# A first attention whose query and value projections move into the tail of a turn, and a feed-forward stage whose first low part is made before the first product is scaled

## The reference

```
x = x + tanh(g_xattn[0]) * window_attention(layernorm(x), ctx)   # 8 heads, window 16, 1x1 projections q, k, v, o
x = x + tanh(g_ffn[0])   * quantized_ffn(layernorm(x))           # int8 fake-quantized w1, gelu, w3
x = x + tanh(g_xattn[1]) * lane_attention(layernorm(x), ctx)     # q = layernorm(x) @ Wq.T, k, v from ctx
x = x + tanh(g_ffn[1])   * swiglu_ffn(layernorm(x))              # with low-rank additions
```

## Time and profile before

| | before |
|---|---|
| median of 3 runs | 3655.55 us |
| lowest, highest | 3651.84, 3661.02 us |
| the profiled execution | 3649.41 us |
| its span | 3647.7 us |
| PE, DVE, ACT, POOL busy | 90%, 39%, 24%, 10% of the span |
| mean granted TensorE clock | 0.954 of full speed |
| first attention | 0 to 475.45 us |
| fused feed-forward and queries | 475.45 us to about 980 us |

### The profile page before, as it was taken

The page is one execution under the profiler, slowest core; times in us unless marked ns, Lnnn a source line. Parts: engine busy times, 40 slices in busy tenths (PEclk is TensorE's granted clock), DMA queues, the critical chain, the costliest instruction groups (busy, mean ns, idle before and its releaser), DMA issues. The chain is left out here.

```text
span 3647.7 us, 52611 instructions
## 1 busy us (share of the span) xinstructions
PE 3294.2 (90%) x21047; PEld 2507.2 (69%) x21076; DVE 1433.3 (39%) x2021; ACT 889.8 (24%) x1232; POOL 349.3 (10%) x304
## 2 busy tenths in 40 slices
PE   5888855999799997899999669999999999999999
PEld 2454442777678885566666458888888888778777
DVE  6666657777220002677676362111121122310000
ACT  1222243333121112555454221111111111200000
POOL 2000000000000001232222111111111111000000
PEclk9999977999789998999999879999999999999999
DMA  4656451221232223121121243222222222544443
GB/s 95 131 115 126 89 185 35 70 70 59 76 104 69 61 60 110 70 85 58 64 80 63 66 131 103 91 94 94 94 94 94 94 94 82 202 145 132 141 141 104
DMA packets 339441, 352.61 MB, mean 97 GB/s; under 512 B 154352, under 2 KB 261472, under 8 KB 337264
## 3 DMA queue, kind: packets, MB, share of 16 engines
q1 hardware_dynamic: 339312, 350.79, 31.1%
HBM read 215.23 MB, written 126.97 MB: 94 GB/s over the span
## 5 line engine op out<-in xcount | busy, mean ns | idle before, releaser
L2213 PE MATMUL g_ps<-g_xs,g_wt 128*128 128x512 f32 x4128 | 957.2, 392 | 0.0
L2213 PEld LDWEIGHTS g_ps<-g_xs,g_wt 128*128 128x128 f32 x4128 | 774.3, 189 | 160.7
L2269 PE MATMUL g_ps<-g_wd,g_h 128*128 128x512 f32 x2016 | 463.0, 392 | 6.8 <-DMA g_h<-g_hidden 4.1
L2269 PEld LDWEIGHTS g_ps<-g_wd,g_h 128*128 128x128 f32 x2016 | 381.1, 189 | 88.1 <-DMA g_h<-g_hidden 4.7
L2131 DVE SCALAR_TENSOR_TENSOR g_act_out<-g_ps,g_g,g_act_out 128x512 f32<-128x512 f32 (+1 forms) x88 | 66.1, 751 | 691.4 <-ACT g_act_out L2063 691.4
L2063 ACT ACTIVATE g_act_out<-g_ps 128x512 f32<-128x512 f32 (+1 forms) x88 | 52.6, 598 | 655.7 <-PE g_ps L2213 655.7
L1263 PE MATMUL kv_gps<-kv_xh,kv_wh 128*128 128x512 f32 x512 | 200.5, 392 | 0.0
L1263 PE MATMUL kv_gps<-kv_xl,kv_wh 128*128 128x512 f32 x512 | 199.3, 389 | 0.0
L1263 PE MATMUL kv_gps<-kv_xh,kv_wl 128*128 128x512 f32 x512 | 199.3, 389 | 0.0
L1008 PE MATMUL f_gps<-f_xt,f_qwh 128*128 128x256 f32 x1024 | 194.2, 290 | 1.4 <-DVE f_xt L887 1.4
L1611 PEld LDWEIGHTS a_tps<-a_ident,a_e 128*128 128x128 f32 x1024 | 113.4, 144 | 104.6 <-issue 90.5
(11 more groups left out here) (247 smaller groups left out, 4257.6 us busy)
## 6 DMA issues: line engine op xcount, KB each, us to landing
g_h<-g_hidden SPq DMA_DIRECT2D x176, 256.0 KB, 2.6
g_hidden<-g_h SPq DMA_DIRECT2D x84, 512.0 KB, 2.7
kv<-kv_y SPq DMA_DIRECT2D x16, 1024.0 KB, 5.7
a_kv<-kv SPq DMA_DIRECT2D x16, 1024.0 KB, 4.9
g_xb<-x SPq DMA_DIRECT2D x24, 512.0 KB, 4.0
g_down<-g_raw SPq DMA_DIRECT2D x22, 512.0 KB, 2.8
g_raw<-g_down SPq DMA_DIRECT2D x22, 512.0 KB, 4.3
g_raw<-in_L_ffn_gate_w_dram SPq DMA_DIRECT2D x21, 512.0 KB, 4.0
```

The costliest lines, as they stand in the source:

```text
L2213: w = pe.matmul(gps[:, c % 2, m, :], wt[m][i][:, l, ks], xs[c][:, r, k, :], start=(k == 0 and a == 0), stop=(k == NK - 1 and a == 2))
L2269: w = pe.matmul(to, tile[:, p % RING, l, cols], wd[f][:, r, os], start=(f == 0 and a == 0), stop=False)
```

## The change

In the first attention, PE makes only the two key projections at the head of a turn, between the first scores; the two query projections come after the last `attend`, the values after the transposes of the output, and the product by `Wo` (now a function `final`) last. ACT follows that order, and its exponential comes after the copy of the output instead of before. DVE runs `normalize` between the maxima (`largest`) and their subtraction (`shift`); its two `value` steps move from between the selects to before and after `sums`. SP spreads the keys ahead of the store of the values. In the fused stage, `low(b - 1, 0)` stands ahead of `scale_h(b + 1)`, and `low(b - 1, 1)` ahead of `with_bias(b + 2)`.

```diff
@@ -184,8 +184,8 @@
                 if b >= -1 and there(b + 3):
                     load_cond(b + 3)
                 if there(b + 2):
+                    spread_keys(b + 2)
                     store_values(b + 2)
-                    spread_keys(b + 2)
                     spread_values(b + 2)
             store(B - 1)
             sp.wait_ge(S["out"], 16 * B)
@@ -260,20 +260,21 @@
                          ).then_inc(S["sa"], 1)
 
             for b in range(-2, B):
-                for i in range(4):
-                    if there(b + 2):
-                        (query, key)[i // 2](b + 2, i % 2)
+                for t in range(NK):
+                    if there(b + 2) and t < 2:
+                        key(b + 2, t)
                     if there(b + 1):
-                        middle(b + 1, i)
-                if there(b + 1):
-                    for t in range(4, NK):
                         middle(b + 1, t)
-                    act.wait_ge(S["sub"], b + 2)
-                    act.activation(sc[:, :, :, :], sc[:, :, :, :], ACT.Exp, scale=SCALE).then_inc(S["ex"], 1)
+                if there(b + 2):
+                    for a in range(2):
+                        query(b + 2, a)
                 if there(b):
                     act.wait_ge(S["ot"], b + 1)
                     past(act, "wo", b)
                     act.copy(o[:, :], tps[:, :]).then_inc(S["oe"], 1)
+                if there(b + 1):
+                    act.wait_ge(S["sub"], b + 2)
+                    act.activation(sc[:, :, :, :], sc[:, :, :, :], ACT.Exp, scale=SCALE).then_inc(S["ex"], 1)
 
         @block.vector
         def _(dve):
@@ -331,9 +332,11 @@
                 dve.tensor_tensor(vt[:, 4 * a:4 * a + 4, :], prj[:, :].rearrange("p (k c) -> p k c", c=P),
                                   bvr[:, :].unsqueeze(1).to_broadcast([P, 4, P]), ALU.add).then_inc(S["sbv"], 1)
 
-            def shift(n):
+            def largest(n):
                 dve.wait_ge(S["sel"], NK * n + NK)
                 dve.tensor_reduce(mx[:, :], scu, AX.X, ALU.max).then_inc(S["mx"], 1)
+
+            def shift(n):
                 dve.wait_ge(S["mx"], n + 1)
                 dve.tensor_tensor(scu, scu, mx[:, :].unsqueeze(2).to_broadcast([P, NK * H, W]), ALU.subtract).then_inc(S["sub"], 1)
 
@@ -363,16 +366,20 @@
                 for t in range(NK):
                     if there(b + 1):
                         select(b + 1, t)
-                    if there(b + 2) and t in (4, 7):
-                        value(b + 2, t // 7)
+                if there(b + 1):
+                    largest(b + 1)
+                if there(b):
+                    normalize(b)
                 if there(b + 1):
                     shift(b + 1)
-                if there(b):
-                    normalize(b)
                 if there(b + 3):
                     stats(b + 3)
+                if there(b + 2):
+                    value(b + 2, 0)
                 if there(b + 1):
                     sums(b + 1)
+                if there(b + 2):
+                    value(b + 2, 1)
                 if there(b + 3):
                     norm(b + 3)
                 if there(b):
@@ -383,17 +390,17 @@
             def project(n, i, a):
 
                 if i == 0:
-                    past(pe, "sbv", 2 * n) if a == 0 else pe.wait_ge(S["sbq"], 2 * n + 1)
+                    pe.wait_ge(S["sbk"], 2 * n + 2) if a == 0 else pe.wait_ge(S["sbq"], 2 * n + 1)
                     pe.wait_ge(S["xn"], n + 1)
                     src = xn[:, 512 * a:512 * a + 512]
                 else:
-                    pe.wait_ge(S["sbq"], 2 * n + 2) if a == 0 else pe.wait_ge(S["sbk"], 2 * n + 1)
+                    past(pe, "sbv", 2 * n) if a == 0 else pe.wait_ge(S["sbk"], 2 * n + 1)
                     pe.wait_ge(cl[n % 2], 16 * (n // 2) + 16)
                     src = cond[:, n % 2, 512 * a:512 * a + 512]
                 pe.matmul(prj[:, :], w4[:, i, :], src, start=True, stop=True).then_inc(S["pq" if i == 0 else "pk"], 1)
 
             def values(n, a):
-                pe.wait_ge(S["sbk"], 2 * n + 2) if a == 0 else pe.wait_ge(S["sbv"], 2 * n + 1)
+                pe.wait_ge(S["sbq"], 2 * n + 2) if a == 0 else pe.wait_ge(S["sbv"], 2 * n + 1)
                 for k in range(4):
                     m = pe.matmul(prj[:, P * k:P * k + P], cond[:, n % 2, P * (4 * a + k):P * (4 * a + k) + P], w4[:, 2, :],
                                   start=True, stop=True)
@@ -437,6 +444,8 @@
                 for t in range(NK):
                     m = pe.transpose(tps[:, P * t:P * t + P], on[:, P * t:P * t + P], ident[:, :])
                 m.then_inc(S["ot"], 1)
+
+            def final(b):
                 pe.wait_ge(S["oe"], b + 1)
                 for c in range(2):
                     m = pe.matmul(pvp[:, 512 * c:512 * c + 512], w4[:, 3, :], o[:, 512 * c:512 * c + 512], start=True, stop=True)
@@ -448,20 +457,27 @@
             for b in range(-2, B):
                 if there(b):
                     turn(b)
-                for i in range(4):
-                    if there(b + 2):
-                        project(b + 2, i // 2, i % 2)
-                    if there(b + 1) and i < 3:
-                        scores(b + 1, i)
+                for t in range(3):
+                    if there(b + 2) and t < 2:
+                        project(b + 2, 1, t)
+                    if there(b + 1):
+                        scores(b + 1, t)
                 for t in range(NK):
                     if there(b):
                         attend(b, t)
                     if there(b + 1) and t < NK - 3:
                         scores(b + 1, t + 3)
-                    if there(b + 2) and t in (1, 4):
-                        values(b + 2, t // 4)
+
+                if there(b + 2):
+                    for a in range(2):
+                        project(b + 2, 0, a)
                 if there(b):
                     output(b)
+                if there(b + 2):
+                    for a in range(2):
+                        values(b + 2, a)
+                if there(b):
+                    final(b)
 
 def layer_norm_steps(nc, dve, S, n, src, st, mv, rstd_ready, tag=""):
 
@@ -915,14 +931,15 @@
                 quant_v(b)
                 if b + 2 < B:
                     norm(b + 2)
+
+                if b:
+                    low(b - 1, 0)
                 if b + 1 < B:
                     scale_h(b + 1)
                 if b:
-                    low(b - 1, 0)
+                    low(b - 1, 1)
                 if b + 2 < B:
                     with_bias(b + 2)
-                if b:
-                    low(b - 1, 1)
             result(B - 1)
             stats_y(B - 1)
             norm_y(B - 1)
```

## The result

The changed kernel takes 3565.63 us, the median of 4 executions (3555.67 to 3567.83), against 3656.47 us for the kernel before on the same chip: the ratio is 0.9746, with a 95% interval of 0.9723 to 0.9769. The forecast was 3565 us. The profiled execution took 3563.57 us, its span 3561.9 us. Its mean granted clock, 0.956, is that of before (0.954).

What follows compares the result with a forecast made beforehand. Engines waiting on each other bound the attention turn, none full; the fused stage waited for `low`. Attention 69 us (57 + 10 + 2) plus fused stage 22 gave 91 us saved, 3565 us; range for 8 in 10: 3550 to 3592.

Steps and rivals of the forecast that it cites:

- The turn: First attention: PE's sum over head, middle and tail of a turn is 22.1 us, against 26.37 before.
- The slow product: Last product of an attention turn, sometimes 3.50 instead of 1.98 us; claimed to go, else 1.5 us in about every turn.
- SyncE's loop: First attention, from store of values through spreading, load of x and DVE to next store: 21.2 us, 19.8 to 23.6.
- Rival (1): First attention: a loop other than PE's sets a turn of 24 us; 24 us less gain, 3589 us; chance 0.14.
- the prediction's signs of being wrong: Attention turns: DVE's statistics wait for x, first key projection waits for second `value`, or PE's clock is below 0.95.
- The term of -57: First attention: 14 turns at 22.3 us, 312 against 369 us, save 57 us; bounds 61 and 39.
- The start: First attention before its turns: keys first, turn 0 near 54 instead of 64.3 us, 10 us saved, between 5 and 11.
- The stage's end: First attention, turns 14 and 15: earlier normalization gives 1.2 us, up to 3 with a fast product; 2 us taken.
- The fused stage: Low part moved ahead of the scaling: 1.61 us in eleven full rounds, 2.0 and 2.5 in two early; 22 us, 0 to 27.
- Rival (2): Fused stage keeps its rounds, the later scaling handing the saving back; 22 us less gain, 3587 us; chance 0.08.
- Rival (3): First attention: halts keep PE at 1.2 GHz, a turn grows to about 38 us, total 3785 us, slower; chance 0.03.

Runs made afterwards that it cites:

- attention part alone: The kernel before with only the attention's edits of the change, the fused stage's order as before: 3591.86 us, ratio 0.9833.
- x loaded first: Changed kernel, but SyncE issues the store of the result and the load of x ahead of the spreading of the values: 3557.56 us, ratio 0.9730.
- queries first in block 0: Changed kernel with the four projections of the very first block in the old order on PE and ACT: 3561.34 us, ratio 0.9740.
- fused part alone: The kernel before with only the fused stage's new order: 3629.19 us, ratio 0.9926.
- the kernel with the late keys: Changed kernel with SyncE's order of before, keys spread between the store of the values and their spreading: 3689.86 us, ratio 1.0094.

## Why the prediction was right

The prediction was right in what carries the gain, the new turn and the vanished wait for the low part, and near in the total, where its terms missed in opposite directions: the attention gave 62.1 us for 69, the fused stage 24.6 for 22. That the median lies within 1 us of the forecast is partly luck. The two profiled spans differ by 85.8 us, not 91; the forecast for the profiled execution was 3558, and it took 3563.57. The prediction then added 6.1 us for the distance from a profiled execution to the median, which was 2.1 after the change.

**The turn** was summed as 22.1 us, and is 22.09. Point by point from its head at 191.32: `attend` at 5.04 (forecast 4.95), first query projection 13.62 (13.6), transposes of the output 16.49 (16.4), last product 20.37 (20.3), the second `value` ended at 21.91 (22.1), key projection at 22.96 (23.0). The slow product went, as forecast, in twelve of the fourteen turns with a full tail; the other two are the long ones. In turns 14 and 15, whose tails have no projections to fill them, it took 3.4 us (1.98 in both in the profile of the attention part alone). The prediction spoke of three halts in the new tail; its own points, like the trace, have two.

**The step that missed** is the one on SyncE's loop: 21.2 us with a worst case of 23.6, priced by adding 0.2 us to a turn. In this execution it took 24.5 us once and 23.2 once (from store to store of the values). The first of these is a landing of 5.0 us, 7.3 until x was issued, a landing of 7.2 and 5.0 on DVE; in the second x took 7.5 us to land. The worst case had been added up from the earlier trace rows, whose longest landings are 4.9 and 6.9 us. They cost 4.2 and 2.7 us, of which about 1.1 and 1.0 are the slower last product that the halt brought with it; with 0.5 us of the first turn they make up all that is missing to 22.09. Rival (1) was thus true of two turns in fourteen, and one of the prediction's signs of being wrong did show: DVE's statistics waited for x, four times and 6.0 us in total. The term of -57 measured -52.5, and -59.4 in the profile with x loaded first. Why a landing takes 5.5 us in one turn and 7.5 in another was not found out. The page "DMA: Bandwidth & Descriptors" of the Trainium skill gives the formula by which the loop would have been 18.2 us in its section "Anatomy of one DMA", for DMAs that GpSimd issues; the prediction used it for SyncE's. It does not agree here: behind the spreading x took up to 7.5 us to land, against its 3.2.

**The start** came at 54.14 for 54, with the steps of the sum at their places (block 1's first key 37.09 for 37, block 0's scores 39.10 for 39). But the keys' being first, which stood at the head of that reasoning, is the smaller part of it, as the run with queries first in block 0 showed. **The stage's end** was to give 2 us and cost 0.6: turn 14 was 2.0 shorter as said, but turn 15 until the next stage took 22.3 us instead of 19.7, with a last product of 3.40 us that had been 1.98. In the profile of the attention part alone, with fast last products, this stretch took 40.2 us, 1.8 less than before: the term hangs on the clock.

**The fused stage** was 22 and measured 24.6. From its first `turn_y` to its end it is 376.2 us before and 349.3 after, 27.0 less, and the same 349.3 us with the fused part alone. Full rounds gave 1.80 us instead of 1.61: besides the wait of 1.61, the transposes of the second half now start 0.17 us before the product ahead of them is recorded as ended. The two early ones gave 3.4 us each instead of 2.0 and 2.5: the waits there fell from 3.42 and 4.58 (the longest of the earlier trace rows) to 1.49 and 2.08, and one of the products behind them ran at 3.63 us instead of 4.70. The stretch ahead of that, the preparation of the weights, varies between 129 and 132 us from one kernel's profile to another's, without a pattern that follows the edits; it took back 2.4 us here. Rival (2) did not come true: DVE keeps 2.61 us of idle time in front of `result`.

**Rival (3)**, the lower clock, showed itself where PE stood still for longer: 3.26 and 1.79 us in the two long turns, halts of 1.10 to 2.26 us in turns 14 and 15, and 5.8 us in each turn of the kernel with the late keys, which did become slower than before. The prediction's argument against it was weaker than it looked. In the earlier trace rows the 0.7 us between two projections are no halt of PE, which makes scores from 200.64 to 201.49; and its price of 38 us a turn would, by its own factor of 3.34 for 1.82, have been 41. In an ordinary turn the clock is 1.00, and two halts of 0.8 us between products left it up. That is consistent with "TensorE: Matmul & The Clock Gate" of the Trainium skill, section "Part 1": activity lifts it.

## What to carry to other kernels

Fill the waits at a step's end with work whose inputs are long there, and then look at what each moved step lets start: here the queue that issues the DMAs had to be reordered with TensorE, and without that the same change is 1% slower than none. A step moved forward on one engine gives nothing when the next engine's list has another step ahead of its consumer; follow the chain through the lists of all engines. Where a queue must wait for a landing, put the loads that have nothing to wait for in front of that wait. And price the first rounds of a pipeline apart: an order that is better in the full rounds can lose as much in those without their full work.

## What the runs showed of the hardware

A halt can cost more than its length. The scores of 128 positions took 1.51 us instead of 0.85 after 5.79 us of idle TensorE, and the last product 3.00 instead of 1.88 in the turn that had waited 3.26 us. Halts of 1.35 and 1.10 us between the last `attend` and the last product still left it at 3.3 to 3.7 us in six of sixteen turns, while two halts of some 0.8 us with products between them left the clock at 1.00 and every last product at 1.88. Halts alone do not decide it: in the kernel before, the same 2.20 and 1.10 us stand in front of last products of 3.50 us (granted clock 0.56) and of 1.98 us (1.00), and what decides between them was not found out. And the same load of 512 KB landed in 4.5 to 7.5 us (median 5.5) when issued behind eight DMAs of small pieces on its queue, in 5.0 to 5.9 us (median 5.7) ahead of them.
